# A moved product of the state-space scan, an earlier input load, a norm inside the scan, and output stores inside the last layer

## The reference

```
def mamba(x):                       # x is first normalised over its features
    xz = x @ W_in + b_in;  gate = x @ W_gate + b_gate         # 256 channels
    a = silu(causal_conv(xz, 4 taps))
    delta = softplus(a @ W_delta + b_delta);  B = a @ W_B;  C = a @ W_C    # B, C: 16 states
    for t: h = exp(delta_t * A) * h + (delta_t * a_t) * B_t;  y_t = sum_n h * C_t
    return (y + a * D_skip) * silu(gate) @ W_out + b_out
x1 = x + mamba(norm(x))
z = norm(x1)
for each of 6 layers:               # windowed attention with rotary q and k, then a gated FFN
    z = z + attention(shift(z));  z = z + ffn(layernorm(shift(z)))
out = x1 + z
```

## Time and profile before

| | us |
|---|---|
| median of 3 runs (lowest, highest) | 3793.05 (3788.48, 3798.14) |
| the profiled execution: its own time | 3797.34 |
| its span, first to last instruction | 3795.5 |
| PE busy | 3526.2 (93%) |
| DVE busy | 3139.4 (83%) |
| ACT busy | 2647.5 (70%) |
| POOL busy | 2423.3 (64%) |

### The profile page before, as it was taken

The page is one execution under the profiler, slowest core; times in us unless marked ns, Lnnn a source line. Parts: engine busy times, 40 slices in busy tenths (PEclk is TensorE's granted clock), DMA queues, the critical chain, the costliest instruction groups (busy, mean ns, idle before and its releaser), DMA issues.

```text
span 3795.5 us, 148907 instructions
## 1 busy us (share of the span) xinstructions
PE 3526.2 (93%) x61280; PEld 2227.8 (59%) x61280; DVE 3139.4 (83%) x4377; ACT 2647.5 (70%) x4972; POOL 2423.3 (64%) x2197
## 2 busy tenths in 40 slices
PE   5677676899999999999999999999999999999997
PEld 2222222466666666666666666666666666666664
DVE  4899998788888888888878888788888888888883
ACT  4545454677777777777777777777777777777775
POOL 0356555676666666666667676667676666666661
PEclk9889899899999999999999999999999999999998
DMA  3000000011111111111111111011111111111111
GB/s 78 0 0 0 0 0 0 26 34 30 32 37 49 37 32 32 32 49 37 37 33 32 43 43 38 28 32 32 49 41 34 32 32 49 38 37 32 32 32 34
DMA packets 64426, 120.18 MB, mean 32 GB/s; under 512 B 18196, under 2 KB 35986, under 8 KB 63634
## 3 DMA queue, kind: packets, MB, share of 16 engines
q1 hardware_dynamic: 63762, 110.70, 10.0%
HBM read 20.50 MB, written 2.10 MB: 6 GB/s over the span
## 4 chain that ended last, share of the span: by engine, by line
POOL 32%; issue 26%; PE 23%; DVE 1%; ACT 1%; POOLq 1%; DMA 0%; DVEq 0%; ACTq 0%; SPq 0%
POOL arena L501 18%; POOL arena L508 8%; POOL arena L515 6%; PE qk L1132 5%; PE trb L1004 3%; PE ob L1193 3%; PE vob L1201 3%; PE vob L1138 2%; PE sc L1220 2%; PE sc L1169 2%; PE ob L1004 1%; PE sc L1227 1%; PE sc L1163 0%; PE vob L1243 0%; POOL arena L484 0%
## 5 line engine op out<-in xcount | busy, mean ns | idle before, releaser
L508 POOL TENSOR_TENSOR arena<-arena,rnorm 128x512 f32<-128x512 f32 x768 | 786.5, 1046 | 904.0 <-ACT rnorm L627 903.4
L501 POOL TENSOR_TENSOR arena<-arena 128x512 f32<-128x512 f32 x768 | 963.9, 1278 | 36.5 <-DVE arena L889 36.4
L634 ACT ACTIVATE arena<-trb 128x512 f32<-128x512 f32 x768 | 462.6, 602 | 412.9 <-PE trb L1004 412.8
L1132 PE MATMUL qk<-wqkv,xs 128*128 128x512 f32 x1536 | 732.6, 600 | 17.9 <-issue 10.6
L888 DVE TENSOR_TENSOR arena<-qk,tab_q 128x512 f32<-128x512 f32 x384 | 263.5, 686 | 414.7 <-ACT arena L620 407.3
L484 POOL TENSOR_TENSOR arena<-arena 128x512 f32<-128x512 f32 x256 | 300.3, 1183 | 344.3 <-DVE arena L860 328.8
L1004 PE MATMUL trb<-ident,arena 128*128 128x128 f32 x3072 | 483.8, 280 | 14.6 <-ACT arena L634 6.9
L1132 PEld LDWEIGHTS qk<-wqkv,xs 128*128 128x128 f32 x1536 | 293.8, 192 | 311.6 <-issue 295.6
L894 DVE TENSOR_REDUCE ssq<-arena 128x16 f32<-128x1024 f32 x384 | 463.9, 1208 | 0.0
L620 ACT ACTIVATE arena<-qk 128x512 f32<-128x512 f32 x768 | 426.9, 587 | 46.7 <-PE qk L1132 34.1
L1004 PEld LDWEIGHTS trb<-ident,arena 128*128 128x128 f32 x3072 | 347.2, 141 | 147.0 <-issue 99.2
(11 more groups left out here) (139 smaller groups left out, 5862.5 us busy)
## 6 DMA issues: line engine op xcount, KB each, us to landing
arena<-arena SPq DMA_DIRECT2D x192, 384.0 KB, 3.2
arena<-arena SPq DMA_DIRECT2D x192, 64.0 KB, 3.0
wqkv<-in_L_ffn_Wqkv SPq DMA_DIRECT2D x18, 512.0 KB, 3.7
wo<-in_L_ffn_Wo SPq DMA_DIRECT2D x6, 512.0 KB, 5.5
arena<-in_L_attn_x SPq DMA_DIRECT2D x8, 256.0 KB, 2.8
out<-arena SPq DMA_DIRECT2D x8, 256.0 KB, 2.2
w<-in_L_ffn_W SPq DMA_DIRECT2D x6, 341.0 KB, 3.0
arena<-in_sel SPq DMA_DIRECT2D x1, 1024.0 KB, 5.2
```

The costliest lines, as they stand in the source:

```text
L501: nc.gpsimd.tensor_tensor(ts[c * 2 + j][:, heads], tu[:, 0, heads], tu[:, 1, heads], ALU.add).then_inc(summed[0], 1)
L508: nc.gpsimd.tensor_tensor(part, part, rnorm[j][:, 8 * h:8 * h + 8].unsqueeze(2).to_broadcast([P, 8, HEAD]), ALU.mult) \
L634: A((qT, kT)[j][u][:, 4 * h:4 * h + 4, at_col:at_col + P], TRB.rearrange("p (a t) -> p a t", a=4), ACT.Copy) \
L1132: MM(QK[:, 512 * h:512 * h + 512], lhsT=xs[u][:, c * P:(c + 1) * P], rhs=wqkv[:, col:col + 512], start=True, stop=True) \
```

## The change

1. **Load.** x is loaded first, in eight buffers (`x_tokens`, in the room of `act[0]`), with only `ident` ahead; the other 25 constants follow. PE, DVE and ACT wait for the constants only ahead of `mamba_in`.
2. **Product.** For odd n, the product of m = 1 is made by GpSimd, from `b_sb`, a copy of bank 0 that ScalarE makes. DVE makes the other three of each two states. The scan of (n odd, m = 1) moves behind the two products of the next state; that of n = 15 stands at the group's end.
3. **Norm.** The second norm of group g - 1 is done inside the scan of group g: `mean_of` on PE at the end of iteration 13, `centre_output` at the head of VectorE's state 14, `square_of` on ScalarE in state 14, `var_of` on PE in iteration 15, `root_of` on ScalarE at the group's end, `scale_output` after `gate`. The last group's is done behind the scan.
4. **Stores.** The last layer's slots run to 86; after the slots 67, 68, 69, 70, 71, 74, 80 and 86 each engine does its part of one group's output. In the drain three loads of ScalarE's function table fall away.

```diff
+FINAL = {67: 0, 68: 1, 69: 2, 70: 3, 71: 4, 74: 5, 80: 6, 86: 7}
...
+        x_tokens = [act[0][:, g * GROUP:(g + 1) * GROUP].rearrange("p (c f) -> p c f", f=DIM) for g in range(GROUPS)]
...
+        b_sb = cut(GROUP)
+        pxc, psq, prstd = (cut(GROUP) for _ in range(3))
...
+            sp.dma_start(ident[:], t["ident"]).then_inc(ident_in[0], 16)
+            for g in range(GROUPS):
+                sp.dma_start(x_tokens[g], x_rows[g * GROUP:(g + 1) * GROUP, :].rearrange("(c p) f -> p c f", p=P)).then_inc(x_in[g][0], 16)
             with nc.allow_non_contiguous_dma("small parameters, once"):
                 for dst, src in small:
                     sp.dma_start(dst, src).then_inc(const_in[0], 16)
...
             def scan_group(g):                                  # GpSimd
                 for n in range(D_STATE):
+                    if n % 2:
+                        k = n * MT + MT - 1
+                        item(pool, b_kept, g * (D_STATE // 2) + n // 2)
+                        item(pool, dx_done, g * MT + (MT - 1))
+                        item(pool, scan_done, g * (D_STATE * MT) + (k - NH_BUF)) if k >= NH_BUF else None
+                        nc.gpsimd.tensor_tensor(dbx[k % NH_BUF], dx[MT - 1], b_sb, ALU.mult).then_inc(dbx_pool[0], 1)
                     item(pool, c_kept, g * D_STATE + n)
...
             def scan_group(g, first, last):                     # ScalarE
...
                     A(a3[:, :, 1:], d3[:, :, 1:], ACT.Exp, scale=a_neg[:, m, n:n + 1]).then_inc(dA_done[0], 1)
+                    if m == 0 and n % 2:
+                        item(act_e, dbx_done, g * PRODUCTS + (products(n) - 1))
+                        slot(act_e, dbx_pool, g * (D_STATE // 2) + n // 2)
+                        A(b_sb, bank[0][:], ACT.Copy).then_inc(b_kept[0], 1)
...
+                    if k == NORM_AT * MT + MT - 1 and not first:
+                        square_of(g + -1)
+                if not first:
+                    root_of(g + -1)
...
+            def centre_output(j):                               # VectorE
+                item(dve, p_mean, j)
+                item(dve, mo_used, j)
+                V.tensor_tensor(pxc, x1T[:, ds(j * GROUP, GROUP)], bank[7][:], ALU.subtract).then_inc(p_xc[0], 1)
...
+                    if n == NORM_AT and not first:
+                        centre_output(g + -1)
+                    if n % 2 == 0 and n:
+                        products_of(g, n, range(MT))
+                        scan_of(g, n - 1, MT - 1)
+                        for m in range(MT):
+                            scan_of(g, n, m)
+                    elif n % 2:
+                        products_of(g, n, range(MT - 1))
+                        scan_of(g, n, 0)
...
+                scan_of(g, D_STATE - 1, MT - 1)
                 if not last:
                     inputs(g + 1)
                 gate(g)
+                if not first:
+                    scale_output(g + -1)
...
                 def spread_b(n):                                # TensorE
-                    pe.wait_ge(dbx_done[0], g * steps + (n + 1) * MT)
+                    pe.wait_ge(dbx_done[0], g * PRODUCTS + (products(n - 1) if n else 0) + MT)
+                    if n:
+                        pe.wait_ge(b_kept[0], g * (D_STATE // 2) + n // 2 + 1)
...
                     if 0 <= n - BC_AT < MT and not last:
                         bc_product(g + 1, n - BC_AT)
+                    if n == NORM_AT - 1 and not first:
+                        if not last:
+                            item(pe, z_pos, (g + 1) * MT + 1)
+                        mean_of(g + -1)
+                    if n == NORM_AT + 1 and not first:
+                        var_of(g + -1)
...
+            def with_final(l, k):                               # TensorE; the others likewise
+                layer_slot(l, k)
+                g = final_at(l, k)
+                if g is not None:
+                    item(pe, f_sum, g)
+                    item(pe, roped, LAST_UNIT * 2 + 1)
+                    slot(pe, f_ready, g)
                     for c in range(GROUP // P):
+                        last = turn(bank[g % 2][:, c * P:(c + 1) * P], fin[g % 2][:, c * P:(c + 1) * P], start=True, stop=True)
                     last.then_inc(f_turned[0], 1)
```

More of the change, by code:

```diff
@@ L53, in layer_slots, with final_at @@
             body(l, k)
-    for k in range(TURN, LAYER - PER_GROUP + LAG_DOWN + 1):
+    for k in range(TURN, max(FINAL) + 1):
         body(DEPTH - 1, k)
+def final_at(l, k):
+    return FINAL.get(k) if isinstance(l, int) and l == DEPTH - 1 else None
 def unit_at(l, k, lag):
@@ L412, in _ @@
             load_w2(0)
+            out_rows = out.rearrange("s n f -> (s n) f")
             def transfer_slot(l, k):
@@ L587, in prepare, with square_of, root_of @@
                     A(zlog[m], zexp[m], ACT.Ln, bias=1.0).then_inc(z_log[0], 1)
+            def square_of(j):
+                item(act_e, p_xc, j)
+                A(psq, pxc, ACT.Square).then_inc(p_sq[0], 1)
+            def root_of(j):
+                item(act_e, p_var, j)
+                slot(act_e, p_out, j)
+                A(prstd, bank[7][:], ACT.Ln, bias=eps[:, 0:1]).then_inc(p_log[0], 1)
+                item(act_e, p_log, j)
+                A(prstd, prstd, ACT.Exp, scale=-0.5).then_inc(p_rstd[0], 1)
             def scan_group(g, first, last):
@@ L685, in layer_slot @@
                 up0, up1 = group_at(l, k, LAG_UP[0]), group_at(l, k, LAG_UP[1])
-                if up0 or up1:
+                drain = isinstance(l, int) and l == DEPTH - 1 and k >= LAYER - PER_GROUP + LAG_UP[0]
+                if up0 or up1 and not drain:
                     act_e.preload_act_table(ACT.Gelu)
@@ L720, in layer_slot @@
                     v_evac(value[0], value[3:], value[2])
-                if up0 or up1:
+                if (up0 or up1) and not drain:
                     act_e.preload_act_table_set(EXP_LN_SET)
@@ L870, in _ @@
             add_output(GROUPS - 1)
-            item(dve, mo_used, GROUPS - 1)
-            plain_norm(GROUPS, xT)
+            centre_output(GROUPS - 1)
+            scale_output(GROUPS - 1)
             def layer_table(layer, c, j):
@@ L1004, in turn @@
                 return MM(out_, lhsT=in_, rhs=ident[0:k, 0:k], is_transpose=True, **kw)
[L1006 to L1016 removed]
+            pe.wait_ge(ident_in[0], 16)
+            for g in range(GROUPS):
+                pe.wait_ge(x_in[g][0], 16)
+                for c in range(GROUP // P):
+                    last = turn(bank[g][:, c * P:(c + 1) * P], x_tokens[g][:, c, :], start=True, stop=True)
+                last.then_inc(x_turned[0], 1)
+            pe.wait_ge(cleared[0], 1)
             def norms_of(i, g0):
@@ L1058, in bc_product, with output_product @@
                     mm.then_inc(bc_done[0], 1)
-            def output_product(g, m, after):
+            def output_product(g, m, after, log=None):
                 if m == 0:
                     item(pe, z_pos, after * MT + 1)
+                    if log is not None:
+                        slot(pe, p_log, log)
                 item(pe, g_done, g * MT + m)
```

216 lines of the change are left out of this document (114 added, 102 removed).

## The result

Four runs of the changed kernel gave a median of 3771.84 us (3769.98 to 3776.87), four of the kernel before 3793.91; the ratio is 0.9945, with a 95% interval of 0.9927 to 0.9962. It is faster by some 22 us, where 28 were forecast (3765), and inside the range of 3748 to 3784. Measured once more, beside the last experiments, it came to 0.9951 [0.9938, 0.9965], which is 16.6 us.

The account below looks back on a forecast made before the run. DVE was taken to bound the scan and PE the layers. The terms -21.0 -37.4 +9.8 +7.2 +29.9 +4.2 -13.4 -10.1 +3.2 sum to -27.6, giving a forecast median of 3765.4 us, range 3748 to 3784.

Parts of the forecast that it names:

- Load: Start of the kernel: with x issued first the norm starts at 12.6 instead of 33.56 us, -21.0 (15 to 23).
- Norm behind the scan: After the scan only one group's norm is left instead of eight: -13.4 us (12.7 to 13.6).
- Behind the last add: End of the kernel: only one group's output remains, 5.0 us instead of 15.1, -10.1.
- The centring: Scan: DVE waits for PE's mean, 3.8 us in groups 1 to 6, 2.9 in group 7; with work +29.9.
- The group's end: Scan, n = 15: the last scan waits 0.9 us for GpSimd's product in eight groups, +7.2.
- The refill of bank 0: Scan: DVE's products wait 0.2 us at 49 places for PE's B spread after ScalarE's copy, +9.8 (5 to 22).
- The dA waits: Scan: waits for ScalarE's dA, 11.1 us, from PE's slow start and softplus pieces, no change (-4 to +8).
- The drain: Last layer's slots: output work inserted there delays DVE and PE, +3.2 us (1 to 8).
- No wait at the centring: Rival, scan: PE is ahead at n = 13, so 29.9 becomes 4.2 and the time 3740; chance 0.08.
- GpSimd becomes the bound: Rival, scan: GpSimd's mean operation passes 1.29 us, 50 us more, 3816; chance 0.04.
- The rhythm stays 6.85: Rival, scan: product, copy and spread take 1.65 us, eating each pair's gain; 24.6 more, 3790; chance 0.14.
- Ends pay less: Rival, start and drain: load held at 12 by 512-byte descriptors, drain costs 7; 3778; chance 0.10.

Follow-up runs that it names:

- two of these mended: The changed kernel with the mean issued in iteration 12 and ScalarE's copy of C behind the dA of half 1: 3743.36 us, 0.9868.
- GpSimd's product first: The changed kernel with DVE's single product ahead of the previous state's scan and GpSimd's product ahead of its C product: 3773.48 us, 0.9949.
- the experiment with the stores: The changed kernel with all eight output groups handled behind slot 85, none within the slots of the drain: 3786.74 us, 0.9978.

## Why the prediction was right, and where its steps were off

**Right in sign, size and most terms, with some luck in the sum.** By stage the forecast missed by -2.3, +11.2, -0.9, -5.7 and -0.3 us; that this adds up to only 2.0 is luck, for the misses have different causes. Load: -23.3 for -21.0, and the 2 us between are the norm behind a busy PE, which the prediction named as its bound of 23. Norm behind the scan: -14.3 for -13.4. Behind the last add: -10.4 for -10.1. The centring: 24.2 us of waits in groups 1 to 7 for 25.7 (3.58 and 2.67 for 3.8 and 2.9), and its cause was shown by moving the mean one iteration up: 24.1 us came back. The group's end: 0.88 to 1.06 for 0.9. (Of the 54 us that were to come back the wait for the mean was 25.7, a little under half, and not the "more than half" of the prediction.) GpSimd did not become the bound (47.27 busy us of 68.86), and scans were not stretched by it, 1194 to 1225 ns. This is as the Trainium skill has it (SBUF — State Buffer, "Who interferes with whom"), since a scan has one operand in PSUM. The warning of the Trainium skill against moving work between these engines (Perfetto Trace Analysis, "Optimizing Scalar/DVE Operations") came true in the outcome, since the moved product cost 5 us of the scan as built. But its reason, the shared port, is not what the runs show: the scans kept their lengths (1194 to 1225 ns, 1193 to 1224 before), the gain went into waits behind in-order queues, and with two of these mended the move gains 8.5 us of the scan.

**The refill of bank 0: mechanism wrong, and a size near it by luck.** +9.8 was taken for 49 waits of products for PE. They were 0.9 us in all. In their place a scan directly behind its own product starts 0.69 to 0.76 us behind the product's start instead of 0.58, which is some 8.5 us (48 times 0.12 and 16 times 0.17). Putting a scan between them took it away. The refill became a wait once other waits were gone: 6.8 us with GpSimd's product first and 6.6 with the copy of C late.

**The dA waits: the mis-sized term.** The prediction put them down to PE's slow start in a group and to the softplus pieces, with "no change, -4 to +8". That was wrong: they rose from 11.1 to 22.2 us. At twelve more places (states 9 and 11 in groups 1 to 6) the scan starts 0.15 us late, again 0.19 us behind the end of its dA as at the waits of these groups, but too little for the view to list: 1.8 us more. ScalarE's queue was counted by its work, which fits, and not by whom each entry waits for. The copy of C waits for PE's `spread_c`, PE's iteration now waits for the copy of bank 0, and dA of half 1 is behind both. With all products on VectorE they are 10.1 us, with the copy of C moved there is none. This term of +11 to 13 is why the scan grew by 24.9 instead of 13.7.

**The drain: +3.2 predicted, -1.2 measured** (61.6 to 60.3 us), but 61.6, no change, in the repeat. The chain did lengthen where it was said to: the scores of slot 68 start 1.37 us behind the hidden product instead of 0.25. A stop of PE in these scores, which no term had, came on top (2.08 us for 0.41). But PE's half-clock stretches near the end are gone. Three groups of four up products took 2.56, 3.68 and 3.68 us before (timeline of PE) and 2.00, 1.93 and 1.97 after, and that alone is 4.0 us:

```profile
3764.16 2.56 PE L1220 MATMUL sc<-xnT,w 128*128 128x512 f32 x4 [2.03 <-DVE xnT L978]
3767.58 3.68 PE L1220 MATMUL sc<-xnT,w 128*85 128x512 f32 x4 [0.87 <-ACT xnT L679]
3772.20 3.68 PE L1220 MATMUL sc<-xnT,w 128*128 128x512 f32 x4 [0.94 <-DVE hid_last L924]
```

Why they are gone is open, as the experiment with the stores shows.

**The rivals.** "No wait at the centring" and "GpSimd becomes the bound" are ruled out by the waits and windows above. "The rhythm stays 6.85" is ruled out by 6.41 to 6.44 where nothing else is in the way. "Ends pay less" is wrong: both paid more. So the gain forecast at the product, 37.4 us, did not arrive. 24.2 us went into the wait for the mean, 12.9 into dA, 8.5 between product and scan, 0.9 into bank 0 and 7.6 into the groups' ends, and 4.2 and 4.2 are the work of centring and scaling: -37.4 + 62.5 = +25.1, against 24.9 measured. The gain that was measured comes from the two ends: x first, the norm behind the scan, and the stores.

**Left open.** What the 0.12 and 0.17 us between a product and its own scan are made of was not isolated, nor why they are longer in the first and the last group. Nor is it shown why the layer phase differs by up to 8 us between kernels that agree there, and what set the clock at the end of the kernel before.

## What to carry to other kernels

Before work is taken off the engine that bounds a stage, follow each new dependency through the in-order queue of every engine that it passes, and ask what stands behind the waiting entry: here one index (when PE issues a mean) was worth 24 us, and one place in ScalarE's queue some 10, more than the product that was moved. A small helper should be issued one iteration earlier than its consumer's order suggests. Look at the two ends of the program as carefully as at its loops: the order of one DMA queue was worth 11.9 us in the trace, more than half of the gain that was measured.

## What was not expected of the hardware

- A scan that directly follows the product it reads starts 0.69 to 0.71 us after the product's start at 48 places and 0.75 to 0.76 at 16; a scan that follows a product which it does not read starts 0.58 to 0.60 after it, where nothing else is late.
- GpSimd's product of two 128 x 512 float32 tiles took 1268 to 1286 ns at each of 64 places, the C products with the same shapes 1090 to 1287 in the kernel before.
- In the drain the granted clock of PE was 0.68 over the last 16 us before the last add in the kernel before. With 0.6 us of transposes in some of PE's gaps it was 1.00 in ten traces and 0.89 in two; without them, in the one kernel that puts the stores at the end, 0.89.
- At 3716.3 us of the kernel after, TensorE's queue stands 2.08 us in the scores (L1264) with nothing in the profile that ended it. Such a stop of 1.5 to 2.4 us is at this place in all ten traces of kernels with the product on GpSimd, and in none of the three with all products on VectorE; the kernel before has 0.41 us. The same drain took 60.3 to 61.8 us with the stop and 58.0 to 59.8 without it. The cause was not isolated.
